# A six-block decoder layer pair: the last, ternary feed-forward in rounds of two sequences with 512-column products, its input state handed over through DRAM

## What is computed

```
def _L1_ffn_ref(x, w1_w, w1_s, w2_w, w2_s, h1_w, h1_s, h2_w, h2_s, w3_w, w3_s):
    h = silu(tlin(x, w1_w, w1_s)) * tlin(x, w2_w, w2_s)      # 256 -> 1024
    h = gelu(tlin(h, h1_w, h1_s))                            # 1024 -> 1024
    h = gelu(tlin(h, h2_w, h2_s))                            # 1024 -> 1024
    return tlin(h, w3_w, w3_s)                               # 1024 -> 256
x = layernorm(x + _L1_ffn_ref(x, ...))                       # tlin(x, w, s) = (x @ w.T) * s
```

## Time and profile before

| | us |
|---|---|
| median of 3 runs | 2042.75 (2038.22 to 2046.46) |
| profiled execution: span from its first to its last instruction | 2047.7 |
| PE busy (matmuls, pipelined) | 1796.9 (88%) |
| DVE / ACT / POOL busy | 1181.8 / 987.0 / 461.0 |
| ternary feed-forward, from its first matmul to the end | 1336.6 to 2047.7 |

### The profile page before, as it was taken

How to read it: one execution, slowest core, us unless ns; L and a number is a source line. 1 busy time by engine, 2 the same in 40 slices (tenths; PEclk the granted TensorE clock), 3 DMA queues, 4 the chain that set the end, 5 groups by cost and what they waited for, 6 DMA issues and landing times. The chain is left out here.

```text
span 2047.7 us, 39500 instructions
## 1 busy us (share of the span) xinstructions
PE 1796.9 (88%) x14845; PEld 1598.2 (78%) x14940; DVE 1181.8 (58%) x2467; ACT 987.0 (48%) x1964; POOL 461.0 (23%) x747
## 2 busy tenths in 40 slices
PE   2699999967999999578859969959999999999998
PEld 2577777756788887445549969959999999999998
DVE  2466677643676767388856869823444444444443
ACT  1367776641555555455546746623333333333331
POOL 3633443001011111134426845400000000000000
PEclk9899999986999999779979989979999999999999
DMA  5765666507877775260000033030000000000000
GB/s 165 161 142 122 132 136 140 105 25 161 178 166 161 162 161 105 91 228 1 0 1 1 1 106 97 24 117 6 10 20 10 10 10 20 10 10 10 10 16 11
DMA packets 104548, 155.87 MB, mean 76 GB/s; under 512 B 13120, under 2 KB 84800, under 8 KB 100416
## 3 DMA queue, kind: packets, MB, share of 16 engines
q1 hardware_dynamic: 99296, 149.95, 30.4%
q10 hardware_dynamic: 5120, 4.20, 1.1%
HBM read 107.97 MB, written 49.81 MB: 77 GB/s over the span
## 5 line engine op out<-in xcount | busy, mean ns | idle before, releaser
L2130 ACT ACTIVATE ffn_slots<-ps,ffn_sh 128x256 f32<-128x256 f32 x256 | 107.5, 472 | 322.7 <-PE ps L2036 322.4
L2036 PE MATMUL ps<-ffn_uT_hi,h 128*128 128x256 f32 x1024 | 245.5, 283 | 2.4 <-DVE ffn_uT_lo L2190 2.4
L2036 PE MATMUL ps<-ffn_uT_lo,h 128*128 128x256 f32 x1024 | 245.3, 283 | 0.0
L2036 PE MATMUL ps<-ffn_gT_lo,ffn_h 128*128 128x256 f32 x1024 | 243.9, 282 | 0.0
L2036 PE MATMUL ps<-ffn_gT_hi,ffn_h 128*128 128x256 f32 x1024 | 243.8, 282 | 0.0
L2036 PEld LDWEIGHTS ps<-ffn_uT_hi,h 128*128 128x128 f32 x1024 | 193.9, 189 | 2.6 <-DVE ffn_uT_lo L2190 2.6
L2036 PEld LDWEIGHTS ps<-ffn_uT_lo,h 128*128 128x128 f32 x1024 | 193.9, 189 | 0.0
L2036 PEld LDWEIGHTS ps<-ffn_gT_hi,ffn_h 128*128 128x128 f32 x1024 | 192.8, 188 | 0.0
L2036 PEld LDWEIGHTS ps<-ffn_gT_lo,ffn_h 128*128 128x128 f32 x1024 | 192.8, 188 | 0.0
L641 ACT ACTIVATE cross_probs<-ps 128x512 f32<-128x512 f32 x192 | 115.3, 602 | 108.7 <-PE ps L451 70.7
L641 ACT ACTIVATE latent_probs<-ps 128x512 f32<-128x512 f32 x192 | 115.4, 602 | 99.4 <-PE ps L451 55.9
(11 more groups left out here) (432 smaller groups left out, 5334.7 us busy)
## 6 DMA issues: line engine op xcount, KB each, us to landing
latent_split<-latent_qk_hi SPq DMA_DIRECT2D x16, 512.0 KB, 3.1
latent_split<-latent_qk_lo SPq DMA_DIRECT2D x16, 512.0 KB, 4.2
queries<-latent_split SPq DMA_DIRECT2D x32, 256.0 KB, 4.8
keys<-latent_split SPq DMA_DIRECT2D x32, 256.0 KB, 6.4
cross_split<-cross_qk_hi SPq DMA_DIRECT2D x16, 512.0 KB, 3.1
cross_split<-cross_qk_lo SPq DMA_DIRECT2D x16, 512.0 KB, 4.3
queries<-cross_split SPq DMA_DIRECT2D x32, 256.0 KB, 5.1
keys<-cross_split SPq DMA_DIRECT2D x32, 256.0 KB, 6.4
```

Source lines behind the costliest of these rows:

```text
L2036: last = nc.tensor.matmul(out_ap, a, b, start=start and n == 0, stop=stop and n == 1, **kw)
L2130: last = nc.scalar.activation(slots[:, p % 2, a], halved(HIDDEN_BANK + p % 2)[:, a, :], ACT.Gelu, scale=scales[:, 2 * p + a:2 * p + a + 1])
```

## The change

Rounds are of two sequences (8 rounds, written out for all engines). A product of the gates, the ups and the two hidden layers has 512 columns and fills a PSUM bank; there are half as many. `gate` and `up` take banks 0 to 3, the hidden chunks the same four banks, the turned state banks 4 and 5, the output 6 and 7. `hT` holds four chunks of eight, and the down products of chunk c (still 256 columns of `w3`) follow the second layer's chunk c+2; those of the last two chunks follow chunks 0 and 1 of the next first layer. `gT` lies where `core.X` lay; so the full attention stores each state to DRAM (`x_mid`), and the feed-forward loads it twice, for the transposes and for the residual. The first two states are copied to `x_plus` inside the full attention, and the verdict on the weights is made there. The wait on `s3` is apart from that on the other scales.

```
@@ full_attention, sync
-                for i in range(2, B):
-                    sp.wait_ge(cT_ready, i - 1)
-                    sp.dma_start(c_in[i % 2][:], ctx_dram[i]).then_inc(ctx_in[i % 2], 16)
+                for i in range(2, B + 5):
+                    if i < B:
+                        sp.wait_ge(cT_ready, i - 1)
+                        sp.dma_start(c_in[i % 2][:], ctx_dram[i]).then_inc(ctx_in[i % 2], 16)
                     if i - 2 < len(core.early):
                         sp.dma_start(f32(core.early[i - 2][0]), core.early[i - 2][1]).then_inc(core.early_in, 16)
+                    if i >= 5:
+                        sp.wait_ge(normalized, i - 4)
+                        sp.dma_start(core.x_mid[(i - 5) // 2][:, (i - 5) % 2 * TT * D:((i - 5) % 2 + 1) * TT * D], core.X[:, i - 5, :]).then_inc(core.x_stored, 16)
+                    if i == 6:
+                        sp.dma_start(core.x_plus[:].rearrange("p t d -> p (t d)"), core.X[:, 0:2, :].rearrange("p b n -> p (b n)")).then_inc(core.x_first, 16)
@@ feed_forward, tensor
+                def hidden_chunk(general, tile, source, o):
+                    for c in range(IT):
+                        last = two_parts(general, ps[:, HIDDEN_BANK + o % 4, :], tile[:, c, o * P:(o + 1) * P], halves(source, ALL, c), 1, c == 0, c == IT - 1)
+                    last.then_inc(hidden_raw, 1)
...
+                    for j in range(ROUNDS):
+                        pe.wait_ge(hidden_split, first_chunk(j) + IT)
+                        for o in range(IT):
+                            second_hidden(general, j, o)
+                            if o >= 2:
+                                down_products(general, j, o - 2)
+                        if j + 1 < ROUNDS:
+                            pe.wait_ge(u_split, IT * (j + 2))
+                        for o in range(IT):
+                            if j + 1 < ROUNDS:
+                                first_hidden(general, j + 1, o)
+                            if o < 2:
+                                down_products(general, j, IT - 2 + o)
+                        if j + 2 < ROUNDS:
                             turn_state(j + 2)
-                        pe.wait_ge(y_taken, j + 1)
...
+                            gate_and_up(general, j + 2)
...
                 pe.wait_ge(core.early_in, 16 * len(core.early))
-                pe.wait_ge(ones_ready, 1)
-                nc.tensor.matmul(ps[0:1, Y_BANK, 0:PIECES], ones[:], core.differing[:], start=True, stop=True).then_inc(counted, 1)
+                used = nc.values_load(core.inexact[:], engines=(mybir.EngineType.PE,), min_val=0, max_val=1)
                 turn_state(0)
-                pe.wait_ge(judged, 1)
...
@@ feed_forward, scalar and vector
-                    nc.scalar.copy(xT[0][:], halved(XT_BANK)).then_inc(xT_hi, 1)
+                    nc.scalar.copy(xT[0][:], turned_state()).then_inc(xT_hi, 1)
-                act.wait_ge(scales_in, 80)
+                act.wait_ge(scales_in, 64)
...
+                def scale_output(j):
+                    dve.wait_ge(down_raw, j + 1)
+                    dve.wait_ge(out_scale_in, 16)
+                    if j >= 1:
+                        dve.wait_ge(stored, 32 * j)
+                    nc.vector.tensor_mul(rows[:], output(), s3[:].unsqueeze(1).to_broadcast([P, TILES, D])).then_inc(y_taken, 1)
+                    row_work = {2: scale_output, 3: add_residual, 4: statistics, 6: normalize}
+                    for o in range(IT):
+                        if j + 1 < ROUNDS:
+                            split_hidden(first_chunk(j + 1) + o, gT, o)
+                        if o in row_work:
+                            row_work[o](j)
+                    if j + 2 < ROUNDS:
+                        split_state(j + 2)
+                        u_chunks(j + 2)
```

More of the change, by code:

```diff
@@ L2111, in split_state @@
                     act.wait_ge(x_turned, i + 1)
-                    nc.scalar.copy(xT[0][:], halved(XT_BANK)).then_inc(xT_hi, 1)
-                def gate_pair(i, p):
-                    act.wait_ge(gate_raw, PAIR * i + p + 1)
-                    if p >= 2:
-                        act.wait_ge(u_ready, PAIR * i + p - 1)
-                    for a in range(2):
-                        last = nc.scalar.activation(gate[:, 2 * (p % 2) + a], halved(GATE_BANK + p % 2)[:, a, :], ACT.Silu, scale=s1[:, 2 * p + a:2 * p + a + 1])
-                    last.then_inc(gated, 1)
@@ L2122, in u_pair_hi @@
-                def u_pair_hi(i, p):
-                    act.wait_ge(u_ready, PAIR * i + p + 1)
-                    nc.scalar.copy(uT[0][:, 2 * p:2 * p + 2], slots[:, p % 2]).then_inc(u_hi, 1)
-                def hidden_pair(p, raw, scales, free):
-                    act.wait_ge(hidden_raw, raw)
-                    act.wait_ge(pair_split, free)
-                    for a in range(2):
-                        last = nc.scalar.activation(slots[:, p % 2, a], halved(HIDDEN_BANK + p % 2)[:, a, :], ACT.Gelu, scale=scales[:, 2 * p + a:2 * p + a + 1])
-                    last.then_inc(activated, 1)
@@ new lines, in u_chunk_hi, with gate_chunks, hidden_chunk @@
+                def u_chunk_hi(i, m):
+                    act.wait_ge(u_ready, IT * i + m + 1)
+                    nc.scalar.copy(uT[0][:, m], u_slots[:, m % 2]).then_inc(u_hi, 1)
+                def gate_chunks(i):
+                    gate_chunk(i, 0)
+                    for m in range(IT):
+                        if m + 1 < IT:
+                            gate_chunk(i, m + 1)
+                        u_chunk_hi(i, m)
+                def hidden_chunk(n, o, scales):
+                    act.wait_ge(hidden_raw, n + 1)
+                    if n >= 2:
+                        act.wait_ge(hidden_split, n - 1)
+                    nc.scalar.activation(hidden_slots[:, n % 2], ps[:, HIDDEN_BANK + o % 4, :], ACT.Gelu, scale=scales[:, o:o + 1]).then_inc(activated, 1)
@@ L2161, in _ @@
             @block.gpsimd
             def _(pool):
-                with pool.Fori(0, B) as j:
-                    rstd_steps(nc, core, pool, mean_ready, rstd_ready, j, TT)
+                for j in range(ROUNDS):
+                    rstd_steps(nc, core, pool, mean_ready, rstd_ready, j, TILES)
                     pool.drain()
@@ new lines, in statistics, with normalize @@
+                def statistics(j):
+                    dve.drain()
+                    for t in range(TILES):
+                        nc.vector.bn_stats(core.stats[:, t, :], rows[:, t, :])
+                    dve.drain()
+                    for t in range(TILES):
+                        last = nc.vector.bn_aggr(core.moments[:, t, :], core.stats[:, t, :])
+                    last.then_inc(mean_ready, 1)
+                def normalize(j):
+                    dve.wait_ge(rstd_ready, j + 1)
+                    for t in range(TILES):
+                        last = nc.vector.tensor_scalar(rows[:, t, :], rows[:, t, :], core.moments[:, t, 0:1], core.rstd[:, t:t + 1], ALU.subtract, ALU.mult)
+                    last.then_inc(normalized, 1)
```

341 lines of the change are left out of this document (157 added, 184 removed).

## The result

In 11 runs beside 11 of the kernel before, the changed kernel takes 2038.91 us (2033.66 to 2043.07), the kernel before 2046.46 (2038.22 to 2051.32): a ratio of 0.9968, 95% interval 0.9957 to 0.9978. By the ratio that is 6.5 us faster, where 28.5 were forecast: clear of the noise, and yet within the 0.5% that the prediction called no change. The profiled spans are 2047.7 and 2038.1 us. They differ by 9.6, of which 3.2 lie ahead of the full attention, in stages that the change leaves alone.

What follows compares the result with a forecast made beforehand. TensorE, never idle from 1400 to 2000 us, was taken to bound the last stage. Products, turns, clock, pipeline ends and start: -52.8 + 15.9 + 9.6 + 7.3 - 8.5 = -28.5 us, median 2042.75 to about 2014, range 1998 to 2040.

Steps and rivals of the forecast that it cites:

- I take 0.217: Last stage: each float32 product of 512 columns costs 0.217 us, the bfloat16 price, against 0.2376 for two of 256.
- at 512 the load should disappear under the stream: TensorE products: loading weights sets a floor near 0.11 us, hampers streaming at 256 columns and is hidden at 512.
- a spacing of 0.225 or more: Starts of 512-column products on TensorE this many us apart would prove the predicted sum wrong; 0.217 was expected.
- Rival 1: 512-column products keep the excess seen at 256 columns: 0.2254 us each, saving 31.3, net -7.0, 2036 us; chance 0.18.
- Rival 2: Products priced by the column, 0.2376 us at 512, float32 streaming slower than bfloat16: nothing saved, 2067 us, slower; chance 0.10.
- Rival 3: TensorE's clock holds over the seven stalls of the last stage: 11.2 us less, 2003 us; chance 0.14.
- Rival 4: Full attention: POOL comes late, 1 to 2 us in each of ten slots, 2024 to 2034 us; chance 0.08.
- products: Last stage: 5120 products of 256 columns at 0.1188 us become 2560 of 512 at 0.217, saving 52.8 us.
- Turns: TensorE idles 2.6 us before the gates while the turned state is split, six times, plus 0.3 at a seventh: +15.9.
- Stall between the last rounds and tail: Between rounds 7 and 8 TensorE idles 2.15 us, last down products wait 0.3, wider final DVE steps add 3.2.
- Start: Start of the last stage: the 7.02 us wait on `s3` goes, `values_load` and branch stay; -8.5 including 1.8 of clock.
- The clock: TensorE's clock falls behind idle times: 1.6 us lost at each of six turns, +9.6; one fall fewer at the start, 1.8.

## Why the prediction was wrong

**The failed step is "I take 0.217"** for a product of 512 columns, and behind it "at 512 the load should disappear under the stream", which took it for granted that the stream itself runs as it does in bfloat16. Measured are 0.2312 as the mean of 2560: 36 us of the 52.8 never came, and the prediction's own sign of a wrong sum, a spacing of 0.225 or more, is there. The reasoning was half right. A weight load does set a floor of 0.111, and it does add to the price of 256 columns (114 with weights of 64, 120 with 128). It also disappears at 512. But there rounded float32 streams at 0.2267 at best, 0.0097 above the 0.217 taken over from bfloat16: that is 25 us of the 36. The earlier trace rows are bfloat16 and could not show it., taken as the far end, pointed the right way. The second part, 6.6 ns on 1536 of the products or 10 us, hangs on where the change allotted `w1`, `w2` and `h1`, and no row of before could price it.

**The rivals.** Rival 1 (a constant excess, 0.2254, 2036 us) named a time 3 us off, by luck: its price was too low by 15 us and its clock too dear by 11. Rival 2 (0.2376) had the cause in the right place, a slower stream, and the size too high. The forecast would have turned into a loss from 0.2281 by its own sum, and 0.2312 lies beyond that; the clock and the start kept it from one. For the same reason it is luck that 2038.91 lies inside the stated 1998 to 2040. Rival 3 (the clock holds) came true behind six of seven turns, not behind the stall between the last rounds. Rival 4 did not occur.

**The terms**, forecast and measured, without the clock: products -52.8, -16.5. Turns +15.9, +15.1. Stall between the last rounds and tail +5.7, +5.8. Start -6.7, -9.9: the read of the verdict did not "stay". What the prediction held for the cost of `values_load` and the branch was the wait for a packet of code (so the queue's name says, and the 1.6 us from its landing to the first gate in four traces), and turn and split now cover it. The clock +9.4, of which -1.8 at the start; measured -2.2 in all. The hand-over 0, 0. The errors: +36.3, -11.6 for the clock, -3.2 for the start, about 21 us of the 22.

**What the clock goes by is open.** Stalls of the same length brought it down behind two of eight in the changed kernel, and behind eight of eight with products 3% faster. That looks as if the pace counted, but with the products in halves, no faster, it fell behind five of eight. With the read of the verdict moved, products and later stalls are those of the changed kernel, only begun 5.4 us earlier, and there it fell behind the fourth turn instead of the third. So neither the length of a stall nor the pace ahead of it decides alone, and when in time a stall falls counts too; no run here separates more. Each of these counts is from one profiled execution.

## What to carry over

Before joining products to save their fixed part, run one series of the new shape in the very type, with the very tiles: the price of bfloat16 (216 ns) did not stand for that of rounded float32 (227 to 234). When a change moves allocations, compare where weights and moving tile lie modulo 256 bytes. A step that prepares the next pair belongs several chunks ahead, not next to its use, and a broadcast of a small tensor never behind megabytes of weights: here these two edits were worth 19.5 and 8.8 us, the doubled width 16. A branch early in a stage is best issued ahead of work that covers it: its code came as a DMA packet, which started 3.7 us behind the transposes with the weights in the queues and 1.5 us without.

## What was unexpected of the hardware

- Rounded float32 streams slower than bfloat16 at the full clock: 226.7 ns for 512 columns against 216.
- The same product of 512 columns costs 226.7, 229 or 232 to 234 ns by the distance of its two tiles in SBUF modulo 256 bytes; the kernel's own layers show it (0.227 and 0.233), and 56 words of padding remove it.
- At 256 columns one distance has two prices, 113.3 and 117.8 ns, each steady through a whole series.
- The first product behind a branch started 1.6 us after a 16 KB packet of the queue called instruction had landed, in each of four traces.
- A saving of 10 us in products was all but lost to the clock, 9 us in the profile, as long as stalls of 2.36 us were left behind it, and kept once they were gone. Whether such a stall lets the clock fall changed with a shift of the whole stage by 5.4 us.
